# Order of VectorE's additions and one-hots in the edge-counting stage of a two-layer graph network, and who makes one source one-hot of three

## The chip, the cores and the metric

The kernel runs on one core of one Trainium2 chip. The metric is the device time of one execution in microseconds (us). The engines are TensorE (PE in the rows), VectorE (DVE), ScalarE (ACT), GpSimd (POOL) and SyncE (SP), which issues DMAs. They run side by side and meet at semaphores.

## The reference

1250 nodes with 512 features, 20,000 edges sorted by destination. Two layers, cut to what matters here:

```python
h = relu(layernorm(x))
agg = segment_sum(h[src], dst)                 # layer 0
z = (1 + eps) * h + agg
x = x + h + relu(bn(relu(bn(z @ W1 + b1)) @ W2 + b2))
h = relu(layernorm(x))                         # layer 1
m = mish(mish([h[src], h[dst], edge_attr] @ W1 + b1) @ W2 + b2)
agg = segment_sum(m, dst)
x = x + layernorm_affine(h + mish([h, agg] @ W3 + b3) @ W4 + b4)
```

The change lies in how layer 0's aggregation is prepared. The kernel does not gather rows for it: it counts how many edges run from each node to each node, as a matrix, and later multiplies that matrix with h.

## The kernel before

The kernel's stages follow one another: counting the edges (to about 111 us), the product of counts and features, the two batch-normalised products of layer 0, the tables of layer 1, the edge loop of layer 1 (most of the time), and the output products. Nothing of the product of counts and features starts before all counts are added.

**Counting.** The edges are cut into tiles of 128, four tiles to a group, 40 groups (`GROUPS`). One tile contributes a matrix product of two one-hot matrices: a **source one-hot** (128 edges x 128, which of 128 low source numbers the edge has) and a **key one-hot** (128 edges x 400). The key is the high part of the source number times 40 plus the distance of the destination from the lowest one of its half group; so two tiles (a half) give a 128x400 block of counts in a PSUM bank, and that block is added into `edge_counts` at a column offset that is read from memory into a register.

Who makes what, for each group `n`:
- VectorE makes the key one-hots of three tiles (`MADE` = 3): `key_hots`, line 1638, in 16-bit floats.
- GpSimd makes the source one-hots of the same three: `src_hots`, line 558.
- ScalarE makes both one-hots of the fourth tile, in three operations (lines 1185, 1186, 1192), and in 20 of the groups from n = 8 on also writes a layer-norm row of h (line 1199, `ROWS_AT`).
- TensorE multiplies: two tiles into one bank, two into another (line 798), four matmuls of 400 columns, then raises `counted`.
- VectorE adds the two banks into `edge_counts` (`add_counts`, line 1682). The second addition waits for the first by the semaphore `counts_added`, since their columns can overlap. A register operation (line 1681) precedes each, and one load of two words from `lowest_row` (`load_stretch`, line 1543) precedes the group.

One-hots, banks and registers stand in three slots (`SLOT` = 3): the one-hots of group n may be written once group n-3 is counted. VectorE's loop over n, in order: load the stretch of n; the key one-hots of n+2; the additions of n. Other work is hung into this loop at numbers: layer-norm statistics for the first four n (`ln_stats`, lines 1491 and 1495), their reciprocal at n = 6 (`SCALE_AT`), three sums for the tables at n = 11 (`SUMS_AT`, `table_sums`), a split of h into a high and a low part at n = 12 and 15 (line 1733), a check for wide groups at n = 30 (`ANY_AT`, lines 1749 and 1750), and at n = 37 (`MORE_AT`) a branch for groups that cover more columns (`count_more`), not taken here.

**GpSimd's tables.** Between its source one-hots GpSimd works out, for all groups at once, which node tiles they cover. It does a piece behind the one-hots of n = 3, 5, 7 and 9. Behind n = 11 comes `ranges_of_groups`, which waits for VectorE's three sums, and behind n = 13 `tables_ready`, which raises `range_ready`; SyncE then sends the table through DRAM to where VectorE reads it at n = 30. GpSimd's queue is in order: the one-hots of n = 12 stand behind that wait.

The lines around the sums, of GpSimd and of VectorE:

```python
if n == TABLES_AT + 4 * TABLES_STEP:      # GpSimd, n = 11, behind src_hots(n)
    ranges_of_groups()
...
if n == SUMS_AT:                          # VectorE, n = 11, behind key_hots(n + 2)
    table_sums()
```

Of the kernel before, what the change touches and what calls it, by code (L numbers as in the profile page):

```python
# [17 lines left out]
ALU = mybir.AluOpType  # L18
# [8 lines left out]
P = 128  # L27
# [3 lines left out]
NP = NT * P  # L31
KD = DIM // P
KH = HID0 // P
GROUP = 4
RING = 4
TILES = -(-EDGES // (GROUP * RING * P)) * GROUP * RING
GROUPS = TILES // GROUP
# [8 lines left out]
HALVES = 2  # L46
DW = 40
KEYS = NT * DW
MADE = GROUP - 1
# [9 lines left out]
SLOT = 3  # L59
# [4 lines left out]
TABLES_AT, TABLES_STEP, TABLES_SUMMED = 3, 2, 18  # L64
SUMS_AT, ANY_AT = 11, 30
# [4 lines left out]
MORE_AT = GROUPS - 3  # L70
# [38 lines left out]
def gnn_kernel(nc, x, src_cols, dst_cols, dst_rows, edge_attr_t, eps, cols, rows, w01, w02,  # L109
               w1, w2, w3, w4, out):  # L110
    ctx = ExitStack()
    with ctx:
# [3 lines left out]
        def sb(name, shape, dt=F32, at=None):  # L116
            size = 2 if dt in (F16, I16) else 4
            for n in shape[1:]:
                size *= n
            if at is None:  # L120
                at = place[0]
                place[0] += size + (-size) % 32
            return nc.alloc_sbuf_tensor_at(name, shape, dt, offset=at), at + size + (-size) % 32
# [82 lines left out]
        KEY, at = sb("key", [P, TILES], at=at)  # L206
# [5 lines left out]
        LO_F, HI_F = SRC_F[:, 0, :], SRC_F[:, 1, :]  # L212
# [10 lines left out]
        KHOT, at = sb("key_onehot", [P, SLOT, MADE, KEYS], F16, at=wa_at)  # L223
        SHOT, at = sb("src_onehot", [P, SLOT, MADE, P], F16, at=at)
# [4 lines left out]
        IOTA_H, at = sb("iota_half", [P, KEYS], F16, at=at)  # L229
# [123 lines left out]
        def sem(name):  # L353
            return ctx.enter_context(nc.semaphore(name))
# [11 lines left out]
        src_ready, key_ready, src_hot, key_hot, hot_act, distance_made = (sem(n) for n in  # L366
            ("src_ready", "key_ready", "src_hot", "key_hot", "hot_act", "distance_made"))
        counted, counts_added, x_added, h0_hi, h0_lo = (sem(n) for n in
            ("counted", "counts_added", "x_added", "h0_hi", "h0_lo"))
# [165 lines left out]
        def _(pool):  # L535
# [17 lines left out]
            def src_hots(n):  # L553
                if n >= SLOT:
                    pool.wait_ge(counted, n - SLOT + 1)
                for j in range(MADE):
                    t = GROUP * n + j
                    ins = nc.gpsimd.tensor_scalar(SHOT[:, n % SLOT, j, :], IOTA[:, 0:P], LO_F[:, t:t + 1], None, ALU.is_equal)
                ins.then_inc(src_hot, 1)
# [7 lines left out]
            def lowest_and_highest():  # L567

                pool.wait_ge(extremes_made, 2)
                table(nc.gpsimd.tensor_copy(RNG_G[:, R_MIN:R_MIN + HALVES], LOW2[:, :]))  # L570
                table(nc.gpsimd.tensor_scalar(ENDS[:, 0:1], LOW2[:, 0:1], LOW2[:, 1:2], None, ALU.min))
                table(nc.gpsimd.tensor_scalar(ENDS[:, 1:2], HIGH2[:, 0:1], HIGH2[:, 1:2], None, ALU.max))
                table(nc.gpsimd.tensor_tensor(SPAN[:, :], HIGH2[:, :], LOW2[:, :], ALU.subtract))
                pairs = [GROUPS, HALVES, HALVES * GROUPS]
                table(nc.gpsimd.tensor_tensor(NEAR[:, 0, :, :], LOWS[:, :].rearrange("g (o k) -> g o k", o=1).broadcast_to(pairs),
                                              LOW2[:, :].rearrange("g (h o) -> g h o", o=1).broadcast_to(pairs), ALU.subtract))

            def stretches():

                pool.wait_ge(table_made, steps[0])  # L580
                table(nc.gpsimd.tensor_tensor(WIDTH[:, :], ENDS[:, 1:2], ENDS[:, 0:1], ALU.subtract))
                for h in range(HALVES):
                    table(nc.gpsimd.tensor_scalar(PASSED[:, h, :], NEG_DW[0:GROUPS, 1:MORE_MAX + 1], SPAN[:, h:h + 1], 0.0, ALU.add, ALU.is_ge))
                for k in range(2):
                    table(nc.gpsimd.tensor_scalar(TILES_BELOW[:, k, :], NEG_TILE[:, :], ENDS[:, k:k + 1], 0.0, ALU.add, ALU.is_ge))
                table(nc.gpsimd.tensor_scalar(NEAR[:, 1, :, :], NEAR[:, 0, :, :], 0.0, None, ALU.is_le))

            def first_tiles():

                pool.wait_ge(table_made, steps[0])
                table(nc.gpsimd.tensor_scalar(MULTI[:, :], WIDTH[:, :], float(P), None, ALU.is_ge))
                table(nc.gpsimd.tensor_scalar(ONE_TILE[:, :], WIDTH[:, :], float(P), None, ALU.is_lt))
                table(nc.gpsimd.tensor_scalar(NEXT[:, :], ENDS[:, 0:1], float((NT - 1) * P), None, ALU.is_lt))
                table(nc.gpsimd.tensor_scalar(NEAR[:, 0, :, :], NEAR[:, 0, :, :], -float(DW), None, ALU.is_gt))

            def further_tiles():

                pool.wait_ge(table_made, steps[0])  # L600
                table(nc.gpsimd.tensor_scalar(NEXT[:, :], NEXT[:, :], 2.0, -1.0, ALU.mult, ALU.add))
                table(nc.gpsimd.tensor_tensor(NEAR[:, 0, :, :], NEAR[:, 0, :, :], NEAR[:, 1, :, :], ALU.mult))
                assert steps[0] == TABLES_SUMMED, steps
# [21 lines left out]
            for n in range(GROUPS):  # L625
                src_hots(n)
                if n == TABLES_AT:
                    lowest_and_highest()
                if n == TABLES_AT + TABLES_STEP:
                    stretches()  # L630
                if n == TABLES_AT + 2 * TABLES_STEP:
                    first_tiles()
                if n == TABLES_AT + 3 * TABLES_STEP:
                    further_tiles()
                if n == TABLES_AT + 4 * TABLES_STEP:
                    ranges_of_groups()
                if n == TABLES_AT + 5 * TABLES_STEP:
                    tables_ready()


# [71 lines left out]
            for s in range(SLOTS, EDGE_PAIRS):  # L712
# [7 lines left out]
                if W3_PAIR <= s < W3_PAIR + 2 * W3_PIECES:  # L720
                    n = (s - W3_PAIR) // 2
# [753 lines left out]
        def _(dve):  # L1475
# [59 lines left out]
            range_regs = [[dve.alloc_register(f"dve_range{n}_{j}") for j in range(2 * HALVES)] for n in range(SLOT)]  # L1535
# [93 lines left out]
            link(nc.vector.tensor_copy(MIN_ROW[:, :], lows[0:1, :]))  # L1629
            nc.vector.tensor_copy(LOWS[:, :], lows[0:GROUPS, :]).then_inc(extremes_made, 1)  # L1630

            def key_hots(n):

                if n >= SLOT:
                    dve.wait_ge(counted, n - SLOT + 1)
                for j in range(MADE):
                    t = GROUP * n + j
                    ins = nc.vector.tensor_scalar(KHOT[:, n % SLOT, j, :], IOTA_H[:, :], KEY[:, t:t + 1], None, ALU.is_equal)  # L1638
                ins.then_inc(key_hot, 1)

            dve.wait_ge(pool_const, 4)
            dve.wait_ge(key_ready, 1)
            for n in range(2):
                key_hots(n)

            def counts_at(first):
                return COUNTS[:, :, bass.ds(first, DW)]

            def counted_in(bank):
                return BANKS[:, bank, 0:KEYS].rearrange("p (c w) -> p c w", w=DW)  # L1650

            def counts_more(n, half):

                past = dve.snap(range_regs[0][HALVES + half], min_val=0, max_val=MORE_MAX)
                with dve.If(past > 0):
                    low = dve.snap(range_regs[0][half], min_val=0, max_val=NP - 1)
                    with dve.Fori(0, past) as k:
# [13 lines left out]
                        nc.vector.tensor_tensor(counts_at(first), counts_at(first), counted_in(XBANK), ALU.add).then_inc(xagg_done, 1)  # L1671
                        dve.reg_add(extras, extras, 1)

            def add_counts(n):

                g = n % SLOT
                dve.wait_ge(counted, n + 1)
                for half in range(HALVES):
                    if half or n > 0:
                        dve.wait_ge(counts_added, HALVES * n + half)  # L1680
                    first = dve.snap(range_regs[g][half], min_val=0, max_val=NP - 1)
                    nc.vector.tensor_tensor(counts_at(first), counts_at(first), counted_in(2 * g + half), ALU.add).then_inc(counts_added, 1)  # L1682

            def spare_rows():

# [80 lines left out]

            for n in range(GROUPS):
                load_stretch(n % SLOT, n)
                if n + 2 < GROUPS:
                    key_hots(n + 2)  # L1770
                if n == MORE_AT:
                    count_more()
                if n == SUMS_AT:
                    table_sums()
                if n == ANY_AT:
                    any_range()
                add_counts(n)
                if n < LG:
                    dve.wait_ge(x_in[n], 16)
                    ln_stats(X, n)  # L1780
                if n == SCALE_AT:
                    dve.wait_ge(std_ready, LG)
                    link(nc.vector.reciprocal(RSTD[:, 0:NT], TMP[:, 4, 0:NT]))
                    nc.vector.scalar_tensor_tensor(NBIAS[:, 0:NT], LN_MV[:, 0:NT, 0], -1.0, RSTD[:, 0:NT],
                                                   ALU.mult, ALU.mult).then_inc(scale_ready, LG)
                if n in SPLIT_AT:
                    split_h0(SPLIT_AT.index(n))
# [106 lines left out]
            for q, (a, b) in enumerate(FILLS):  # L1894
# [9 lines left out]
                for nt in range(a, b):  # L1904
                    dve.wait_ge(dve_chain, chain[0] - (b - 1 - nt))
                    ins = nc.vector.bn_aggr(LN_MV[:, nt, :], STATS[:, nt, :])
# [285 lines left out]
```

## Time and profile before

| | us |
|---|---|
| median of 3 runs | 1142.43 (1142.24 to 1142.64) |
| the profiled execution | 1142.65 |
| its span, first to last instruction | 1140.84 |
| first additions of counts | 11.47 |
| cast of the finished counts begins | 110.84 |

How to read it: a row of the timeline has the start and the length of a run of equal instructions on one engine, and in brackets how long the engine had been idle before and what ended that. A row's length is that of the instruction in the engine's pipeline; the next may start before it has ended, so what a cycle takes is read from starts. Instructions of an engine's sequencer (register operations, loads into registers) carry a q behind the engine's name.

### The profile page before, as it was taken

The page shows a single profiled execution, that of the slowest core. Times are in us where ns is not written, and L with a number is a line of the kernel's source. Part 1 is how long each engine was busy: PE and PEld are TensorE (multiplying, and loading weights), DVE is VectorE, ACT ScalarE, POOL GpSimd, SP SyncE. Part 2 cuts the span into 40 slices and gives each one's busy share as a digit, 9 for nine tenths or more (in the row PEclk, how much of TensorE's full clock was granted, in tenths as well). Part 3 has the DMA queues.
Part 4 walks back from the last instruction along what each step waited for, and adds up shares of the span by engine and source line. Part 5 has one row for each costly group of instructions (what it writes and reads, how often), then busy time and mean ns, then how long its engine had stood idle before and what let it go on. Part 6 is the DMA issues. An engine that isn't in the chain of part 4 may idle for free.

```text
span 1140.8 us, 18418 instructions
## 1 busy us (share of the span) xinstructions
PE 1061.1 (93%) x5689; PEld 893.8 (78%) x5690; DVE 875.8 (77%) x1489; ACT 898.0 (79%) x1134; POOL 676.5 (59%) x589
## 2 busy tenths in 40 slices
PE   3565999998999999999999999999999999999897
PEld 1121889998788888888888888888888888888695
DVE  7798626544525388888899899989988888888786
ACT  6795745633621699999999999999999999999584
POOL 8696505000335487767788888888877677660217
PEclk7556999999899999999999999999999999999899
DMA  2000940110165477666676666666666666761002
GB/s 102 8 1 24 194 101 15 48 74 24 69 210 117 89 169 164 133 138 134 138 136 130 138 139 134 136 139 133 133 145 133 135 138 134 140 126 42 1 1 90
DMA packets 61087, 121.40 MB, mean 106 GB/s; under 512 B 7851, under 2 KB 18348, under 8 KB 60918
## 3 DMA queue, kind: packets, MB, share of 16 engines
q0 software_dynamic: 38048, 87.58, 38.9%
q1 hardware_dynamic: 22998, 33.32, 8.8%
q8 instruction: 20, 0.33, 0.1%
q14 instruction: 21, 0.17, 0.0%
HBM read 107.82 MB, written 7.80 MB: 101 GB/s over the span
## 4 chain that ended last, share of the span: by engine, by line
PE 85%; DVE 10%; issue 2%; POOL 1%; ACT 1%; DVEq 1%; ACTq 0%; POOLq 0%
PE banks L1032 12%; PE banks L1027 12%; PE banks L1028 12%; PE banks L932 10%; PE banks L1012 7%; PE banks L1049 6%; PE banks L1006 6%; PE banks L975 5%; PE banks L855 4%; PE banks L994 4%; DVE edge_counts L1682 3%; PE banks L1025 3%; DVE key_onehot L1638 2%; PE banks L1109 2%; PE banks L909 1%
## 5 line engine op out<-in xcount | busy, mean ns | idle before, releaser
L681 POOL DMA_INDIRECT gather_pq<-q_table,dst x157 | 295.6, 1883 | 56.9 <-issue 47.5
L673 POOL DMA_INDIRECT gather_pq<-p_table,src x157 | 173.0, 1102 | 137.2 <-PE banks L1012 84.0
L1027 PE MATMUL banks<-w_lo,h_hi 128*128 128x512 f32 x620 | 241.5, 389 | 0.0
L1028 PE MATMUL banks<-w_hi,h_hi 128*128 128x512 f32 x620 | 241.3, 389 | 0.0
L1032 PE MATMUL banks<-w_hi,h_lo 128*128 128x512 f32 x620 | 166.2, 390 | 0.0
L1028 PEld LDWEIGHTS banks<-w_hi,h_hi 128*128 128x128 f32 x620 | 116.4, 188 | 24.8
L1032 PEld LDWEIGHTS banks<-w_hi,h_lo 128*128 128x128 f32 x620 | 116.4, 188 | 24.2
L1958 DVE SCALAR_TENSOR_TENSOR h_full<-mish_work,banks 128x512 f32<-128x512 f32 (+1 forms) x154 | 98.5, 681 | 46.6 <-ACT mish_work L1336 43.9
L1027 PEld LDWEIGHTS banks<-w_lo,h_hi 128*128 128x128 f32 x620 | 116.5, 188 | 21.9
L1983 DVE SCALAR_TENSOR_TENSOR message<-mish_work,banks 128x1024 f32<-128x1024 f32 x78 | 95.3, 1222 | 8.7 <-ACT mish_work L1360 0.7
L1324 ACT ACTIVATE mish_work<-banks 128x1024 f32<-128x1024 f32 (+1 forms) x77 | 78.7, 1022 | 26.2 <-PE banks L1012 26.2
L1012 PE MATMUL banks<-edge_attr_parts,we_hi 128*128 128x256 f32 (+1 forms) x316 | 94.5, 321 | 2.1 <-DVE edge_attr_parts L1951 2.1
L1993 DVE TENSOR_TENSOR message_lo<-message,message_hi 128x1024 fp32r<-128x1024 f32 x78 | 96.1, 1232 | 0.1
L1006 PE MATMUL banks<-ident,gather_pq 128*128 128x128 f32 x628 | 94.4, 272 | 0.6 <-DMA gather_pq<-q_table,dst 0.3
L1972 DVE TENSOR_TENSOR h_lo<-h_full,h_hi 128x1024 fp32r<-128x1024 f32 (+1 forms) x77 | 93.3, 1212 | 0.0
L798 PE MATMUL banks<-key_onehot,src_onehot 128*128 128x400 f16 x120 | 44.0, 495 | 46.5 <-DVE key_onehot L1638 32.7
L1356 ACT ACTIVATE mish_work<-mish_work 128x1024 f32<-128x1024 f32 (+1 forms) x79 | 83.4, 1056 | 2.5
L1006 PEld LDWEIGHTS banks<-ident,gather_pq 128*128 128x128 f32 x628 | 74.8, 140 | 11.5 <-DVE h_full L1958 0.6
L1332 ACT ACTIVATE mish_work<-mish_work 128x1024 f32<-128x1024 f32 (+1 forms) x77 | 81.4, 1057 | 2.4
L1328 ACT ACTIVATE mish_work<-mish_work 128x1024 f32<-128x1024 f32 (+1 forms) x77 | 81.3, 1056 | 2.5
L1360 ACT ACTIVATE mish_work<-mish_work 128x1024 f32<-128x1024 f32 (+1 forms) x79 | 83.1, 1052 | 0.1
L1352 ACT ACTIVATE mish_work<-mish_work 128x1024 f32<-128x1024 f32 (+1 forms) x79 | 82.4, 1044 | 0.1
(266 smaller groups left out, 2720.2 us busy)
## 6 DMA issues: line engine op xcount, KB each, us to landing
edge_attr<-in_edge_attr_t SPq DMA_DIRECT2D x79, 128.0 KB, 3.6
x_nodes<-h_hi POOLq DMA_DIRECT2D x10, 256.0 KB, 12.4
x_nodes<-h_lo POOLq DMA_DIRECT2D x10, 256.0 KB, 7.9
p_table<-p_stage SPq DMA_DIRECT2D x10, 256.0 KB, 2.0
q_table<-agg_nodes SPq DMA_DIRECT2D x10, 256.0 KB, 2.9
gather_pq<-p_table,src POOLq DMA_INDIRECT x157, 3.9
gather_pq<-q_table,dst POOLq DMA_INDIRECT x157, 5.2
x_nodes<-in_x SPq DMA_DIRECT2D x3, 768.0 KB, 7.0
```

The costliest lines, as they stand in the source:

```text
L673: nc.gpsimd.indirect_dma_start(GP[:, 2 * j + k, :], None, p_tab[:, :], bass.IndirectOffsetOnAxis(ap=SRC[:, 2 * s + k:2 * s + k + 1], axis= ...
L681: nc.gpsimd.indirect_dma_start(GP[:, 2 * j + k, :], None, q_tab[:, :], bass.IndirectOffsetOnAxis(ap=DST[:, 2 * s + k:2 * s + k + 1], axis= ...
L932: mm = pe.matmul(bank, weights[w][:, k, o * P:(o + 1) * P], acts[a](k)[:, nodes], start=(k == 0 and n == 0), stop=(k == kn - 1 and n == 2) ...
L1006: pe.matmul(Z1v[:, c, k * P:(k + 1) * P], GP[:, 2 * slot + k, c * P:(c + 1) * P], IDENT[:, :], is_transpose=True, skip_group_check=True, s ...
L1012: mm = pe.matmul(Z1v[:, c, 0:P * tiles(s)], w[:, c * P:(c + 1) * P], AT_R[:, j, 0:P * tiles(s)], skip_group_check=True, start=False, stop= ...
L1027: pe.matmul(at, h_high(s, j)[:, c, e], W2_LO[:, c, :], start=False, stop=False)
L1028: pe.matmul(at, h_high(s, j)[:, c, e], W2_HI[:, c, :], start=False, stop=False)
L1032: mm = pe.matmul(at, h_low(s, j)[:, c, e], W2_HI[:, c, :], start=False, stop=(c == KD - 1))
L1958: nc.vector.scalar_tensor_tensor(h_full_of(s)[:, at[0], at[1]], z1_work(s)[:, at[0], at[1]], -0.5, Z1v[:, at[0], at[1]], ALU.add, ALU.mult ...
L1972: nc.vector.tensor_tensor(h_low(s, j)[:, :, 0:P * tiles(s)], h_full_of(s)[:, :, 0:P * tiles(s)], h_high(s, j)[:, :, 0:P * tiles(s)].bitcas ...
L1983: nc.vector.scalar_tensor_tensor(MSG[:, :, :], EB[:, :, :], -0.5, z2_out(s, j), ALU.add, ALU.mult).then_inc(msg_full, 1)
L1993: nc.vector.tensor_tensor(MSG_LO[:, :, :], MSG[:, :, :], MSG_HI[:, :, :].bitcast(F32), ALU.subtract).then_inc(msg_lo, 1)
```

## The change

1. GpSimd makes the source one-hots of two tiles of a group instead of three. VectorE makes the third (`src_last`), in 16-bit floats from `iota_half` instead of from the 32-bit `iota`. The semaphore `key_hot` is raised behind it.
2. For n below 37, VectorE's loop no longer makes the key one-hots of n+2 ahead of the wait for group n's counts. It waits for the counts first and then alternates: first addition of n, one key one-hot of n+2, second addition of n, two key one-hots and the source one-hot of n+2. From n = 37 the order is as it was.
3. GpSimd calls `ranges_of_groups` behind n = 15 and `tables_ready` behind n = 17, where it was 11 and 13.

```diff
             def src_hots(n):
...
-                for j in range(MADE):
+                for j in range(MADE - 1):
...
-                if n == TABLES_AT + 4 * TABLES_STEP:
+                if n == SUMS_AT + SLOT + 1:
+
                     ranges_of_groups()
-                if n == TABLES_AT + 5 * TABLES_STEP:
+                if n == SUMS_AT + SLOT + 1 + TABLES_STEP:
                     tables_ready()
...
+            def key_one(n, j):
+                t = GROUP * n + j
+                nc.vector.tensor_scalar(KHOT[:, n % SLOT, j, :], IOTA_H[:, :], KEY[:, t:t + 1], None, ALU.is_equal)
+
+            def src_last(n):
+                t = GROUP * n + MADE - 1
+                nc.vector.tensor_scalar(SHOT[:, n % SLOT, MADE - 1, :], IOTA_H[:, 0:P], LO_F[:, t:t + 1], None, ALU.is_equal).then_inc(key_hot, 1)
+
             def key_hots(n):
 
                 if n >= SLOT:
                     dve.wait_ge(counted, n - SLOT + 1)
                 for j in range(MADE):
-                    t = GROUP * n + j
-                    ins = nc.vector.tensor_scalar(KHOT[:, n % SLOT, j, :], IOTA_H[:, :], KEY[:, t:t + 1], None, ALU.is_equal)
-                ins.then_inc(key_hot, 1)
+                    key_one(n, j)
+                src_last(n)
...
+            def add_between_hots(n):
+
+
+                dve.wait_ge(counted, n + 1)
+                add_half(n, 0)
+                key_one(n + 2, 0)
+                add_half(n, 1)
+                for j in range(1, MADE):
+                    key_one(n + 2, j)
+                src_last(n + 2)
...
             for n in range(GROUPS):
                 load_stretch(n % SLOT, n)
-                if n + 2 < GROUPS:
+                if MORE_AT <= n < GROUPS - 2:
                     key_hots(n + 2)
...
-                add_counts(n)
+                if n < MORE_AT:
+                    add_between_hots(n)
+                else:
+                    add_counts(n)
```

`add_half(n, half)` is the body of the old loop in `add_counts`: the wait for `counts_added`, the register operation and the addition.

On VectorE, one turn of the loop around group 10 and the next one's load, before (ISA is the register operation of line 1681):

```order
L1543 TENSOR_LOAD lowest_row
L1638 TENSOR_SCALAR key_onehot<-iota_half,key 128x400 x3
L1681 ISA
L1682 TENSOR_TENSOR edge_counts<-edge_counts,banks 128x10x40
L1681 ISA
L1682 TENSOR_TENSOR edge_counts<-edge_counts,banks 128x10x40
L1543 TENSOR_LOAD lowest_row
```

The same turn now:

```order
L1544 TENSOR_LOAD lowest_row
L1687 ISA
L1688 TENSOR_TENSOR edge_counts<-edge_counts,banks 128x10x40
L1635 TENSOR_SCALAR key_onehot<-iota_half,key 128x400
L1687 ISA
L1688 TENSOR_TENSOR edge_counts<-edge_counts,banks 128x10x40
L1635 TENSOR_SCALAR key_onehot<-iota_half,key 128x400 x2
L1639 TENSOR_SCALAR src_onehot<-iota_half,src_parts 128x128
L1544 TENSOR_LOAD lowest_row
```

One hot has moved between the additions, two behind them, and the source one-hot stands ahead of the next load.

On GpSimd, from the last piece of the early tables (behind n = 9) to `tables_ready`, before:

```order
L602 TENSOR_TENSOR lowest_near<-lowest_near 40x160
L558 TENSOR_SCALAR src_onehot<-iota,src_parts 128x128 x6
L608 CAST range_groups<-tile_of 40x1
...
L613 TENSOR_SCALAR range_groups<-reached_by 40x2
L558 TENSOR_SCALAR src_onehot<-iota,src_parts 128x128 x6
L618 TENSOR_SCALAR range_groups<-extra_tiles,many_tiles 40x1
```

And now:

```order
L602 TENSOR_TENSOR lowest_near<-lowest_near 40x160
L558 TENSOR_SCALAR src_onehot<-iota,src_parts 128x128 x12
L608 CAST range_groups<-tile_of 40x1
...
L613 TENSOR_SCALAR range_groups<-reached_by 40x2
L558 TENSOR_SCALAR src_onehot<-iota,src_parts 128x128 x4
L618 TENSOR_SCALAR range_groups<-extra_tiles,many_tiles 40x1
```

The six one-hots of n = 10 and 11 ahead of the wait have become twelve, of n = 10 to 15.

## Rows read from the trace of the kernel before

**Rows 1.** Timeline: start, length, engine; additions of n0, n4, n11, n12, n36; cast.

```profile
11.47 1.29 DVE L1682 TENSOR_TENSOR edge_counts<-edge_counts,banks 128x400 f32 x2
...
29.15 1.27 DVE L1682 TENSOR_TENSOR edge_counts<-edge_counts,banks 128x400 f32 x2
...
45.28 1.27 DVE L1682 TENSOR_TENSOR edge_counts<-edge_counts,banks 128x400 f32 x2
...
50.44 1.29 DVE L1682 TENSOR_TENSOR edge_counts<-edge_counts,banks 128x400 f32 x2 [3.04 <-PE banks L798]
...
103.76 1.28 DVE L1682 TENSOR_TENSOR edge_counts<-edge_counts,banks 128x400 f32 x2
...
110.84 1.26 ACT L1229 CAST counts_hi<-edge_counts 128x1280 fp32r<-128x1280 int16 x1 [9.54 <-DVE edge_counts L1682]
```

**Rows 2.** Chain of waits, 60 to 106 us, shares by line.

```profile
by line: DVE edge_counts L1682 47.9%; DVE key_onehot L1638 35.6%; issue 10.4%; DVEq L1681 4.9%; DVE any_more L1749 0.8%; DVEq L1543 0.7%; DVEq L1757 0.7%; DVEq L1759 0.2%; DVE any_more L1750 0.1%
```

**Rows 3.** One stretch: busy us of PE, PEld, DVE, ACT, POOL, clock, DMA.

```profile
60.60:103.70 43.10, 26.99 (x80) 8.11 (x80) 39.24 (x103) 35.93 (x69) 38.76 (x64) 0.63 0.00 1
```

**Rows 4.** Chain of waits, pieces in order: start, length; GpSimd idle.

```profile
42.13 0.13 DVE key_onehot L1638
42.37 0.55 DVE key_onehot L1638 x2
42.92 0.49 DVE edge_counts L1682
43.55 0.55 DVE edge_counts L1682
44.15 0.22 DVE key_onehot L1638
```

**Rows 5.** Timeline, VectorE: an addition and the independent operation behind it.

```profile
33.90 0.57 DVE L1682 TENSOR_TENSOR edge_counts<-edge_counts,banks 128x400 f32 x1
34.39 0.21 DVE L1783 RECIPROCAL rstd<-tmp 128x10 f32<-128x10 f32 x1
```

**Rows 6.** The loads (ns min/median/max), one register operation, the hot at 44.62.

```profile
L1543 DVEq TENSOR_LOAD <-lowest_row x40: 523/528/781, 9.6 to 108.8; - x40
...
L1681 DVEq FUSED_REGOPS  x1: 55/55/55, 44.4 to 44.4; - x1
...
44.62 0.32 DVE key_onehot L1638
```

**Rows 7.** Timeline: GpSimd's wait for the sums and TensorE's for its hots.

```profile
45.43 0.18 POOL L608 CAST range_groups<-tile_of 40x1 int32<-40x1 f32 x1 [8.14 <-DVE reached_by L1743]
...
48.80 1.16 PE L798 MATMUL banks<-key_onehot,src_onehot 128*128 128x400 f16 x3 [6.25 <-POOL src_onehot L558]
```

**Rows 8.** Other work on VectorE: splits, a reduction, a late load.

```profile
L1733 DVE TENSOR_TENSOR h_lo<-h_nodes,h_hi 128x512 fp32r<-128x512 f32 x2 | 1.4, 684 | 0.0
...
90.47 0.42 DVE L1749 TENSOR_REDUCE any_more<-tile_range 1x4 int32<-1x160 int32 x1
...
85.05 0.33 DVEq L1543
```

**Rows 9.** All key one-hots: ns min/median/max, first and last start.

```profile
L1638 DVE TENSOR_SCALAR key_onehot<-iota_half,key x120: 303/338/656, 7.7 to 105.5; 128x400 f16<-128x400 f16 x120
```

**Rows 10.** Timeline, TensorE: the four matmuls of one group.

```profile
97.69 1.16 PE L798 MATMUL banks<-key_onehot,src_onehot 128*128 128x400 f16 x3 [0.53 <-DVE key_onehot L1638]
98.65 0.51 PE L798 MATMUL banks<-both_onehots 128*128 128x400 f16 x1
```

**Rows 11.** Timeline, VectorE: statistics, hots behind a load, a slow trio.

```profile
22.50 1.87 DVE L1491 BATCH_NORM_STATS2 stats<-x_nodes 128x6 f32<-128x512 f32 x3
...
25.00 0.81 DVE L1638 TENSOR_SCALAR key_onehot<-iota_half,key 128x400 f16<-128x400 f16 x3 [0.41 <-issue]
...
35.31 1.58 DVE L1638 TENSOR_SCALAR key_onehot<-iota_half,key 128x400 f16<-128x400 f16 x3 [0.43 <-PE banks L798]
```

**Rows 12.** Chain of waits: twelve matmuls of the next stage, twice.

```profile
112.25 4.31 PE banks L855 x12
...
119.25 2.35 PE banks L855 x12
```

More of the change, by code:

```diff
@@ L1672, in counts_more, with add_half @@
                         dve.reg_add(extras, extras, 1)
+            def add_half(n, half):
+                g = n % SLOT
+                if half or n > 0:
+                    dve.wait_ge(counts_added, HALVES * n + half)
+                first = dve.snap(range_regs[g][half], min_val=0, max_val=NP - 1)
+                nc.vector.tensor_tensor(counts_at(first), counts_at(first), counted_in(2 * g + half), ALU.add).then_inc(counts_added, 1)
             def add_counts(n):
-                g = n % SLOT
                 dve.wait_ge(counted, n + 1)
                 for half in range(HALVES):
[L1679 to L1682, printed above, removed]
+                    add_half(n, half)
+            def add_between_hots(n):
[6 more added lines that the diff above has]
+                src_last(n + 2)
             def spare_rows():
```

## The prediction

> **What bounds the kernel now.** Only the counting stage is changed, so I read that alone: it runs from the first addition at 11.47 us to the cast of the finished counts at 110.84 [rows 1]. Everything later waits for its end. The chain of waits names the engine: between 60 and 106 us the chain is VectorE's additions (47.9%) and VectorE's key one-hots (35.6%) [rows 2]. TensorE is busy 26.99 of 43.10 us there, ScalarE 35.93, GpSimd 38.76, VectorE 39.24 [rows 3]. So what counts is VectorE's **cycle per group**: one load of the stretch, three key hots, two additions.
>
> Next the cycle, piece by piece, where GpSimd stands idle [rows 4]: key hot to next hot 0.24 (42.13 to 42.37), the other two hots and the start of the addition to 42.84 or so, then 0.49 of addition, a gap, 0.55 of addition, a gap, next cycle at 44.15. The cycle is 2.02. Two things in it are idle waiting. The second addition waits for the semaphore of the first: an addition begins 0.71 after the other although whatever is independent of it may begin 0.49 after it (33.90 to 34.39) [rows 5]. And the next cycle's first hot begins 0.60 after the second addition, since the load of the next stretch takes 0.53 [rows 6] and the hots are queued behind it.
>
> Last, where the stage isn't at its cycle. GpSimd's table of ranges waits 8.14 us for VectorE's sums, with the source hots of group 12 queued behind it; TensorE starves 6.25 us and VectorE's additions of group 12 come at 50.44, 3.04 us idle before them, after those of group 11 at 45.28 [rows 1, 7].
>
> **The change part by part.** I use the 40 groups, n = 0 to 39, and the starts of their first additions [rows 1]: n0 11.47, n4 29.15, n11 45.28, n12 50.44, n36 103.76.
>
> *The new cycle.* Addition, one key hot, addition, two key hots, the source hot. Spacings: 0.49 after an addition, 0.24 after a hot. The second addition still needs the first one's semaphore, 0.71 after it; the hot in between fills 0.49 + 0.24 = 0.73, so that wait costs 0.02 at most. The source hot is not in the trace in this form; it has 128 columns where a key hot has 400. Its spacing lies between a third of 0.24, 0.08, and the whole, 0.24; I take the middle, 0.16. Sum: 0.49 + 0.24 + 0.49 + 0.24 + 0.24 + 0.16 = 1.86 against 2.02. The load hides if VectorE's sequencer runs ahead of the engine: issued behind the source hot, but while the second addition still runs. The row for it: the register operation of group 11's addition stands at 44.4, behind three hots and three reductions in the program, while the third hot began only at 44.62 [rows 6]. It had passed four instructions that had not begun; the new order asks it to pass three.
>
> *GpSimd beside it.* Before, the 24 cycles from n12 to n36 take 53.32 us. They hold 2.2 us of other work: two splits of 0.68, of which 0.6 each counts, 0.65 for the two reductions of any_range (0.42 the first), 0.35 for one late load [rows 8]. That leaves 2.13 a cycle, 0.11 over the clean 2.02, with GpSimd making three source hots of 38.76/64 = 0.61 us. The wait shows in the hots too: 303 ns at least, 338 in the median, 656 at most [rows 9]. With two hots on GpSimd I take two thirds of it, 0.08. **New cycle: 1.94 us.**
>
> *The others must keep up.* TensorE: hots made at 97.55, matmuls from 97.69 to 99.16 at half clock [rows 10], then 0.14 from its semaphore to an addition, as between two additions (42.84 + 0.57 to 43.55). VectorE now makes group n+2's hots only after group n is counted, so two cycles must cover 0.14 + 1.47 + 0.14 and one whole chain of VectorE's own, 1.86: 3.61 against 3.88. It fits by 0.27. ScalarE is busy 35.93/20 = 1.80 a group, GpSimd now 2 x 0.61 = 1.22 plus tables. All below 1.94.
>
> *n4 to n12*, before 21.29 us. Now 8 x 1.94 = 15.52, the three reductions of table_sums 0.42 (hots end their spacing at 44.86, addition at 45.28), and the two small operations of the layer-norm scale: 0.92 from 34.39 to 35.31, plus 0.17, because an exposed load is now followed by the register operation and its 0.1 us to the addition instead of by hots. 15.52 + 0.42 + 1.09 = 17.03: **4.25 us gained**. The stall of rows 7 is in it: the table is asked for behind the hots of group 15, and the sums are made by then, since hots 15 need group 12 counted and the sums precede the additions of group 11. What is late next there is nothing but the cycle. The six table operations (45.43 to 46.8) lie beside VectorE; range_ready moves later but is needed only at n30 and at the stage's end.
>
> *n12 to n36*, before 53.32. Now 24 x 1.94 + 2.2 = 48.76: **4.56 gained**.
>
> *n0 to n4*, before 17.68. Four cycles each lose 0.15 by the exposed load (statistics at 22.50, hots at 25.00 with 0.41 idle [rows 11]), 0.6 in all; against that the slow trio of hots at 15.19 may go, 0.9. The first addition stays at 11.47, where TensorE's first group ends. Between -0.6 and +0.3 with the trio kept or gone; a trio as slow stands at 35.31 (1.50 rather than 0.71) [rows 11], and if that goes too, 0.8 more comes back. **0.2 gained**.
>
> *The end*, n36 to 110.84: hots of 39 and a source hot more, nearly hidden behind the loads of count_more: **0.2 lost**.
>
> Sum: 4.25 + 4.56 + 0.2 - 0.2 = **8.8 us**. The profiled execution took 1142.65 (span 1140.84), the median is 1142.43; 8.8 off the median gives 1133.6.
>
> *TensorE's clock.* The next stage starts at half clock: twelve matmuls 4.31 us from 112.25, 2.35 later at full clock [rows 12]. Where the grant falls after an earlier start is open: about one such 1.96 either way. I put 0 and keep 1.9 in the range.
>
> **The rivals.** *The cycle decides, and its break-even can be stated:* 32 cycles carry the 8.8, so 1.94 + 8.8/32 = 2.215 us is the cycle at which nothing is gained.
>
> (a) **The load is exposed.** If the load goes out only when the source hot starts, a cycle has 0.53 + 0.05 + 0.17 = 0.75 where I put 0.16: 2.53 us. 32 x (2.53 - 2.215) = 10.1 us slower, 1152.5. It decides from an exposure of 0.28 on. Against it stands the register operation that ran ahead; for it, the exposed loads after the statistics, but those follow instructions that wait. 5%.
>
> (b) **Hots blocked by GpSimd.** Hots now start after an addition twice a cycle, not once. If each such start waits for the rest of a running GpSimd operation, half of 0.61 at a presence of 1.22/1.94, that is 0.19 each, 0.38 a cycle: 2.24 instead of 1.94, which is 1143. Before, one start at a presence of nearly one would cost 0.3 by this, and the rows bear 0.11. The slow trios show it can happen. 6%, and 3% that it locks in for more of the hots and is slower.
> The Trainium skill (SBUF — State Buffer, "SBUF: two separate sides") states this as a rule: the port pair that VectorE and GpSimd share is locked for a whole instruction, and the other engine blocks. By it the sum would be 1143 rather than 1133.6; the trace shows both, blocked trios and unblocked ones.
>
> (c) **The loop over TensorE and ScalarE bites.** With 0.27 of slack, a ScalarE group with a layer-norm row or a delayed source hot can hold the second pair of matmuls, and VectorE, which now waits at the head of the cycle, stands. A cycle of 2.0 to 2.15 gives 1135.5 to 1140.3. 22%.
>
> (d) **Cleaner than I think**: 1.86, no slow trios, an early full clock: 32 x 0.08 + 0.8 + 1.9 is 5.3 more, 1128.3 at most. 9%.
>
> My forecast, cycle 1.86 to 2.0 (1131 to 1135.5): 55%.
>
> **How the numbers follow.** Predicted 1133.6. The range takes the forecast, (c) and the nearer half of (d): 1130.0 to 1140.0; about 19% lies outside. A measurement tells 0.2%, 2.3 us, from no change. Faster: 55 + 9 + nearly all of (c), 85%. Same: 7%. Slower: (a) and the lock of (b), 8%.
>
> **What would show it.** In the new trace: first additions of neighbouring groups 1.9 to 2.0 apart from group 4 to 36, no hole at group 12, no GpSimd wait for the sums; loads inside the second addition; cast of the counts at 102 us. Wrong if idle time by issue stands before every first addition (a), if hots last 0.6 (b), or if additions wait for matmuls (c); and the sum is wrong in its source-hot term if that operation spaces more than 0.24.

## The result

| | median us | runs |
|---|---|---|
| before | 1142.54 | 1142.24 to 1145.13, 4 runs |
| changed | 1133.50 | 1132.90 to 1133.70, 4 runs |

The ratio is 0.9908, with a 95% interval of 0.9891 to 0.9925: 9.0 us less. The profiled execution of the changed kernel took 1133.70 us, its span is 1131.7 (1140.8 before). The forecast was 1133.6. The two parts that make up that agreement were both off, by about 2 us each and in opposite directions; most of what follows is about them.

### The profile page after: what moved, and what is told of

It is laid out like the page before. It is cut to its first block, busy times and chain, and to the rows that moved or that the text cites. A ratio compares the mean times of both kernels' runs of the same rounds, so it can differ in the third digit from the quotient of the medians.

```text
span 1131.7 us, 18418 instructions
## 1 busy us (share of the span) xinstructions
PE 1063.5 (94%) x5689; PEld 896.5 (79%) x5690; DVE 871.2 (77%) x1529; ACT 896.6 (79%) x1134; POOL 656.5 (58%) x549
## 4 chain that ended last, share of the span: by engine, by line
PE 86%; DVE 9%; ACT 2%; issue 2%; DVEq 1%; POOL 0%; ACTq 0%; POOLq 0%
PE banks L1033 12%; PE banks L1028 12%; PE banks L1029 12%; PE banks L933 10%; PE banks L1013 7%; PE banks L1050 6%; PE banks L1007 6%; PE banks L976 5%; PE banks L856 4%; PE banks L995 4%; DVE edge_counts L1688 4%; PE banks L1026 3%; PE banks L1110 2%; DVE key_onehot L1635 1%; PE banks L910 1%
## 5 line engine op out<-in xcount | busy, mean ns | idle before, releaser
L1325 ACT ACTIVATE mish_work<-banks 128x1024 f32<-128x1024 f32 (+1 forms) x77 | 78.6, 1021 | 26.3 <-PE banks L1013 26.3
L1349 ACT ACTIVATE mish_work<-banks 128x1024 f32<-128x1024 f32 (+1 forms) x79 | 79.2, 1003 | 3.3 <-PE banks L1033 3.3
```

## The profile after

Timeline of the changed kernel: the first additions of n0, n4, n11, n12 and n36, and the cast of the counts (start, length, engine), to be laid beside [rows 1]:

```profile
11.46 0.57 DVE L1688 TENSOR_TENSOR edge_counts<-edge_counts,banks 128x400 f32 x1 [1.67 <-PE banks L799]
...
28.64 0.57 DVE L1688 TENSOR_TENSOR edge_counts<-edge_counts,banks 128x400 f32 x1 [0.59 <-issue]
...
43.52 0.55 DVE L1688 TENSOR_TENSOR edge_counts<-edge_counts,banks 128x400 f32 x1
...
45.37 0.56 DVE L1688 TENSOR_TENSOR edge_counts<-edge_counts,banks 128x400 f32 x1
...
92.48 0.56 DVE L1688 TENSOR_TENSOR edge_counts<-edge_counts,banks 128x400 f32 x1
...
99.72 1.26 ACT L1230 CAST counts_hi<-edge_counts 128x1280 fp32r<-128x1280 int16 x1 [7.26 <-DVE edge_counts L1688]
```

The cast starts at 99.72 instead of 110.84: **the counting stage is 11.1 us shorter**, not 8.8. The hole at n12 is gone (1.85 us from n11 instead of 5.16). The 0.59 us of idle before the addition of n4 is the load and the register operation behind the statistics.

One whole cycle of VectorE, same view:

```profile
60.02 0.56 DVE L1688 TENSOR_TENSOR edge_counts<-edge_counts,banks 128x400 f32 x1
60.50 0.31 DVE L1635 TENSOR_SCALAR key_onehot<-iota_half,key 128x400 f16<-128x400 f16 x1
60.73 0.56 DVE L1688 TENSOR_TENSOR edge_counts<-edge_counts,banks 128x400 f32 x1
61.21 0.55 DVE L1635 TENSOR_SCALAR key_onehot<-iota_half,key 128x400 f16<-128x400 f16 x2
61.68 0.24 DVE L1639 TENSOR_SCALAR src_onehot<-iota_half,src_parts 128x128 f16<-128x128 f16 x1
61.88 0.57 DVE L1688 TENSOR_TENSOR edge_counts<-edge_counts,banks 128x400 f32 x1
```

Starts: 0.48, 0.23, 0.48, 0.47 for two, 0.20: 1.86. VectorE is without a gap. The loads still take their 0.53; this one is issued at 60.9, behind three instructions that hadn't begun, and ends before the next cycle:

```profile
L1544 DVEq TENSOR_LOAD <-lowest_row x1: 527/527/527, 60.9 to 60.9; - x1
...
L1635 DVE TENSOR_SCALAR key_onehot<-iota_half,key x120: 305/314/429, 7.7 to 94.8; 128x400 f16<-128x400 f16 x120
```

The second row answers [rows 9]: minimum, median and maximum of a key one-hot were 303, 338 and 656 ns and are 305, 314 and 429. No key one-hot takes 0.6 us any more. A little is left elsewhere: one source one-hot took 0.51 us, at 34.05.

Busy time by stretch (PE, PEld, DVE, ACT, POOL, then TensorE's granted clock, where 1.00 is full and 0.50 half, then DMA), first of the kernel before, then of the changed one: the start of the next stage up to where its half clock ends, and a piece behind the table products:

```profile
110.80:116.10 5.30, 3.85 (x11) 3.30 (x12) 4.23 (x12) 4.47 (x6) 4.97 (x9) 0.50 0.72 230
...
356.00:359.80 3.80, 3.80 (x28) 3.80 (x28) 3.80 (x7) 1.36 (x3) 3.23 (x2) 1.00 0.45 67
```
```profile
99.70:107.20 7.50, 6.08 (x17) 5.09 (x18) 6.45 (x15) 5.59 (x7) 7.20 (x10) 0.55 0.87 237
...
356.40:359.80 3.40, 3.40 (x16) 3.40 (x15) 0.00 (x0) 1.07 (x2) 2.34 (x3) 0.50 0.95 219
```

Before, the next stage ran at half clock up to 116.1, which covers 3.85 us of its matmuls; now half clock lasts from 100.4 to 107.2, which covers 6.08 us of them, and another half-clock piece of 3.4 us has appeared at 356. That is where the rest of the 11.1 went. The chain of waits follows it; before, then changed (start, length, matmuls):

```profile
112.25 4.31 PE banks L855 x12
...
166.79 60.92 PE banks L932 x420
...
291.45 5.46 PE banks L975 x12
...
367.61 10.36 PE banks L994 x72
379.79 6.89 PE banks L994 x48
```
```profile
101.12 4.61 PE banks L856 x12
106.05 2.96 PE banks L856 x12
...
156.73 60.92 PE banks L933 x420
...
281.40 4.54 PE banks L976 x12
...
356.58 12.02 PE banks L995 x72
370.43 6.89 PE banks L995 x48
```

The lead is 11.13 us at the first matmul of the stage (112.25 - 101.12), 10.06 where the next product starts, 9.36 at 379.79 against 370.43, and 9.1 at the end of the span. In between, it had grown again to 11.0 (first matmul of line 994 at 352.36, of 995 at 341.34), as the half clock around the batch-norm pause (286.7 to 297 before, 274.5 to 284.7 now) covers less of the matmuls behind it: the first twelve of line 976 take 4.54 us where those of line 975 took 5.46.

A caution on the page of the changed kernel: it shows full clock from the start, but its clock records begin only at 86.8 us. The matmuls tell: a group's four take 1.5 us at 60 us, half clock, and 0.84 at 92.7, full clock.

## The experiments

Two theories. **A**: VectorE's cycle decides until another engine is slower; the order takes two idle waits out of it, the source one-hot costs its spacing. **B**: the gain comes from GpSimd, which is relieved of a third of its work and disturbs VectorE less. The second question, on top of them, is who took 2 us back. All kernels are compared with the kernel before on the same chip, whose median there was 1143.8 to 1144.1. "Stage" is the start of the cast of the counts in the one profiled execution, which no later clock can blur. Two kernels were profiled twice, and their stages repeat to 0.2 us (99.72 and 99.75, 98.56 and 98.36); but the same groups can also take a few tenths more in another execution, as in warm_tail below. The edits are shown against the changed kernel, those of source_only and tables_only against the kernel before.

### The parts, one by one

**order_only**: the new order on VectorE alone; the table calls at 11 and 13, and on GpSimd:

```diff
-                for j in range(MADE - 1):
+                for j in range(MADE):
...
-                if n == SUMS_AT + SLOT + 1:
+                if n == TABLES_AT + 4 * TABLES_STEP:
```


> Of the change only the new order of additions and key one-hots on VectorE; GpSimd makes three source one-hots, its tables stay behind n = 11 and 13. Theory A (VectorE's cycle decides): VectorE's own work is 1.70 us a group, so GpSimd with three source one-hots of 0.61 (1.83, plus its tables) sets about 1.87 a group where it runs free; the stall behind the sums at n = 11 stays and is now paid in full, since GpSimd has no lead to give back: 1136 to 1139 us. Theory B (the gain is GpSimd's relief): the order alone brings little, cycle 2.0 or more, 1140 or more.

Measured 1135.13 (1133.83 to 1136.93), ratio 0.9918; stage 101.91. So the order alone gives 8.9 of the 11.1 us. A, though the median is 0.9 below A's 1136 to 1139. The hole at n12 stays (5.21 us from n11). GpSimd with three one-hots keeps up, as its own timeline of this kernel says: eleven without a break, 0.62 each, 1.87 a group:

```profile
61.67 6.86 POOL L558 TENSOR_SCALAR src_onehot<-iota,src_parts 128x128 f16<-128x128 f32 x11
```

**order_tables**: as order_only, but with the later table calls (the changed kernel without the moved source one-hot, so GpSimd makes three).

```diff
-                src_last(n + 2)
...
-                for j in range(MADE - 1):
+                for j in range(MADE):
```


> New order and later tables, but GpSimd still makes all three source one-hots. Theory A: GpSimd's 1.83 plus its tables sets the cycle, 1.86 to 1.9 against 1.86 in the changed kernel: 1133 to 1135.5 us, so the moved source one-hot is worth little. Theory B: the moved one-hot is what pays, and without it 1137 or more with idle time of TensorE before GpSimd's one-hots.

Measured 1132.53 (1129.34 to 1133.91), ratio 0.9890; stage **98.56, 1.2 us earlier than the changed kernel**. The moved one-hot does not pay. (The median is 0.5 below A's range.)

**source_only**: the third source one-hot on VectorE behind the three key one-hots, two on GpSimd; order and tables as before.

```diff
                 for j in range(MADE):
                     key_one(n, j)
+                src_last(n)
```


> Only the third source one-hot moved to VectorE; old order, old places of the tables. Theory A: VectorE's cycle grows by the one-hot's spacing, 0.16 by my sum: 2.18 plus what contention is left, 1144 to 1147 us less one or two for the shorter stall at n = 12, as GpSimd catches up with two one-hots a group. Theory B: relief of GpSimd outweighs it, 1141 or less.

Measured 1145.68 (1145.32 to 1147.36), ratio 1.0017 (1.0005 to 1.0028); stage 113.78, 2.9 later than before. Most cycles are 2.17 to 2.18, that is 2.02 and 0.16. Over the 24 cycles from n12 to n36, less the 2.2 of other work, 0.04 is left on top where the kernel before had 0.11. A: the relief of GpSimd takes 0.07 off a cycle, but the one-hot costs 0.16.

**tables_only**: only the two calls moved.

```diff
-                if n == TABLES_AT + 4 * TABLES_STEP:
+                if n == SUMS_AT + SLOT + 1:
```


> Only the two calls of GpSimd's tables moved to n = 15 and 17. Both theories: the hole at n = 12 goes. By my sum it is worth the 5.15 us cycle of group 12 less a plain one of 2.1, and 0.5 to 1 of late one-hots behind it: 1138.3 to 1139.5 us. A rival: the table work behind n = 15 costs the same later, because GpSimd with three one-hots (1.83 of 2.1) has no room for it: 1141 or more.

Measured 1139.35 (1137.96 to 1142.59), ratio 0.9968; stage 106.91, 3.9 earlier. n11 to n12 takes 2.02 instead of 5.16.

**tables_early**: the changed kernel with the calls back at 11 and 13.

```diff
-                if n == SUMS_AT + SLOT + 1:
+                if n == TABLES_AT + 4 * TABLES_STEP:
```


> The changed kernel with GpSimd's two table calls back behind n = 11 and 13. If the later calls are what closes the hole at n = 12: the sums come at 43.6 us, GpSimd then needs 1.4 for its tables and 1.2 for two one-hots, TensorE 0.15 and 1 to 1.5, so the additions of group 12 come 4.0 to 4.5 behind those of group 11 instead of 1.85, and the stage and the kernel lose 2.0 to 2.7 us against the changed kernel (1133.5), two thirds of what the hole cost with three one-hots. If the relief of GpSimd closes the hole by itself: no loss.

Measured 1136.15 (1135.03 to 1139.21), ratio 0.9938; stage 103.39, 3.7 later; the kernel loses 2.65, inside the range, but the additions of n12 come 4.79 behind those of n11, more than the 4.0 to 4.5 expected. The profile of the hole, in this kernel, GpSimd's relief notwithstanding:

```profile
45.33 2.35 POOL L558 TENSOR_SCALAR src_onehot<-iota,src_parts 128x128 f16<-128x128 f32 x4
46.62 1.16 PE L798 MATMUL banks<-key_onehot,src_onehot 128*128 128x400 f16 x3 [3.69 <-POOL src_onehot L558]
...
48.26 0.57 DVE L1687 TENSOR_TENSOR edge_counts<-edge_counts,banks 128x400 f32 x1 [2.89 <-PE banks L798]
```

The tables wait for VectorE's sums, the one-hots of n12 wait for the tables, TensorE idles 3.69 us, VectorE 2.89. The later calls are needed; two one-hots instead of three don't close it.

Stage ends side by side:

| source one-hot | order before, tables early | order before, tables late | new order, tables early | new order, tables late |
|---|---|---|---|---|
| on GpSimd | 110.84 | 106.91 | 101.91 | 98.56 |
| on VectorE | 113.78 | not run | 103.39 | 99.72 |

The order is worth 8.3 to 10.4, the later tables 3.3 to 3.9, the moved one-hot **costs** 1.2 to 2.9. B falls as the source of the gain.

### The disputed terms of the sum

**source_two**: two of the three source one-hots on VectorE, one on GpSimd.

```diff
-                for j in range(MADE - 1):
+                for j in range(MADE - 2):
...
+                for j in (MADE - 2, MADE - 1):
```


> The changed kernel with two of three source one-hots on VectorE, GpSimd makes one. It measures the term that I put at 0.16 us. If VectorE's cycle is the bound: it grows from 1.86 by one source one-hot's spacing, 0.16 to 0.2, to 2.02 to 2.06, 32 cycles, 5 to 6.5 us more than the changed kernel. If GpSimd's share slows VectorE's hots noticeably, its relief gives part back and the cycle stays under 2.0.

Measured 1138.21 (1136.16 to 1138.85), ratio 0.9950; stage 104.72. The cycle in the timeline, addition to addition:

```profile
60.23 0.56 DVE L1690 TENSOR_TENSOR edge_counts<-edge_counts,banks 128x400 f32 x1
...
61.90 0.41 DVE L1640 TENSOR_SCALAR src_onehot<-iota_half,src_parts 128x128 f16<-128x128 f16 x2
62.22 0.56 DVE L1690 TENSOR_TENSOR edge_counts<-edge_counts,banks 128x400 f32 x1
```

1.99, below the 2.02 to 2.06 expected if nothing came back from GpSimd's relief. But the other spacings are those of the changed kernel's cycle to 0.01 (0.49, 0.23, 0.48, 0.47), so nothing came back; the second source one-hot is cheaper than I took it: two of them space 0.32, where one spaced 0.20 in the cycle shown and 0.16 in others. My 0.16 stands as the mean of two.

**load_exposed**: the changed kernel, but the sequencer must see its source one-hot finished before it issues the next load, n from 5 to 37.

```diff
+                if 5 <= n <= MORE_AT:
+                    dve.wait_ge(key_hot, n + 2)
                 load_stretch(n % SLOT, n)
```


> The changed kernel, but from n = 5 to 37 VectorE's sequencer waits for its own last source one-hot before it issues the load of the next stretch: the prediction's rival (a) made real. If the load is hidden today only because the sequencer runs ahead: each cycle grows from 1.86 by the one-hot's end, its semaphore, 0.53 of load and 0.2 of register operation, less 0.2 of spacing, about 0.8; 32 x 0.8 = 26 us more, 1156 to 1161. If the load is not really hidden today and partly paid already: under 10 us more.

Measured 1160.79 (1160.46 to 1163.18), ratio 1.0144; stage 129.13, 29.4 later. Chain of waits of this kernel between two cycles:

```profile
59.78 0.53 DVEq L1544
60.31 0.05 issue
60.36 0.02 DVEq L1686
60.38 0.05 issue
60.43 0.06 DVEq L1687
60.48 0.05 issue
60.53 0.57 DVE edge_counts L1688
```

0.75 us from the load to the addition, just the exposure that rival (a) was priced with; the cycle is 2.84 (60.53 to 63.37). It shows what the run-ahead of VectorE's sequencer is worth: about 1 us a cycle. The groups without a split of h have the same 2.84. The break-even that I gave, a cycle of 2.215, comes out roughly: (2.84 - 2.215) x 32 = 20, and the kernel is 17 us slower than the one before, its stage 18.3 later.

### Who took 2 us back

**warm_tail**: 16 small matmuls of constants behind the last group, their result unused.

```diff
             for n in range(GROUPS):
                 count_group(n, n % SLOT)
+            for _ in range(16):
+                pe.matmul(BANKS[:, LOW_BANK, 0:P], ONES_R[:, :].bitcast(F32), IOTA[:, 0:P], start=True, stop=True)
```


> The changed kernel with 16 small matmuls of constants (128 columns of 32 bits) on TensorE behind the last counted group, into a bank that nobody reads. In the changed kernel TensorE idles 4.9 us there at full granted clock and the chip falls to half clock from 100.4 to 107.2 us. If that idle stretch is what drops the clock, and the drop is what eats most of the 11.1 us that the counting stage gains: full clock stays over the start of the next stage, 6.1 us at half clock become about 3.3, 2.5 to 3 us less than the changed kernel. If the clock falls for another reason, or the gain is lost elsewhere: no change, or some tenths more because matmuls stand in the queue.

Measured 1132.49 (1131.59 to 1133.95), ratio 0.9902. The stage ended 0.7 us later in the profiled run (100.46), most of it in the groups from 29 to 32, before the added matmuls; why is not shown. And yet that run was 2.1 us faster than the changed kernel's (1131.59 against 1133.70). Its next stage starts with matmuls at full clock, 0.23 and 0.11 apart, where the changed kernel had 0.43 and 0.19 (the row of the added 16 counts 32, two to each):

```profile
97.90 4.36 PE L829 MATMUL banks<-iota,ones 128*128 128x128 f32 x32
102.01 0.48 PE L858 MATMUL banks<-counts_hi,h_hi 128*128 128x512 f32 x1
102.33 0.39 PE L858 MATMUL banks<-counts_hi,h_lo 128*128 128x512 f32 x1
102.56 0.27 PE L858 MATMUL banks<-counts_hi,h_hi 128*128 128x232 f32 x1
102.67 0.28 PE L858 MATMUL banks<-counts_hi,h_lo 128*128 128x232 f32 x1
```

The medians, of two chips, don't separate it from the changed kernel (1133.50), and 1.0 less is not the 2.5 to 3 that I expected. The profile shows only that the half clock at the stage's start and at 356 is gone; what that is worth, order_tables_warm shows below.

**pad_test**: the changed kernel with a clear of 1280 columns ahead of the last additions.

```diff
+                if n == GROUPS - 1:
+                    nc.vector.memset(A_HI[:, 2, 0:1280].bitcast(F32), 0.0)
```


> The changed kernel with one idle clear of 1280 columns on VectorE ahead of the last group's additions, about 1.3 us on the stage's chain, nothing else. If time moves one to one: 1.3 us more. If the granted clock's place is what decides the rest: the following stages start at another place against the chip's changes of clock, and the end moves by something else, 0 to 3 us more, with the half-clock stretches (100 to 107 and 356 to 360) at other places or gone.

Measured 1133.53 (1132.75 to 1136.32), ratio 0.9912. The stage ends 1.73 later (101.45; the clear is 1.1 of it, most of the rest stands in slower cycles of groups 24 to 26), and the profiled run takes 1133.71, as without it (1133.70). Its first twelve matmuls took 4.41 and the next were at full clock at once, and the half-clock piece at 356 is missing:

```profile
102.85 4.41 PE banks L856 x12
107.43 2.35 PE banks L856 x12
```

So the kernel's end does not follow the stage's end one to one: the 1.7 us came back entirely, through the clock.

### The changed kernel again, and a better one

Three kernels on one chip, five, five and four executions. **after_again** is the changed kernel, **order_tables_again** the one with all source one-hots on GpSimd, **order_tables_warm** that one with the 16 matmuls of warm_tail.

> The changed kernel once more, on the chip of the next three kernels. 0.990 to 0.993 of the kernel before; counting stage finished at 99.7 us, whatever the granted clock does behind it.

> The changed kernel with all three source one-hots back on GpSimd, beside the changed kernel. If the moved one-hot is worth nothing (GpSimd's 3 x 0.61 = 1.84 a group against VectorE's 1.86 with it): counting stage finished at 98.6 us against 99.7, and a median 0 to 1.5 us below the changed kernel's. If its one profile on the other chip was luck: the same or above.

> New order, later tables, three source one-hots on GpSimd, and 16 small matmuls of constants on TensorE behind the last counted group. If both findings add up: 1.2 us from the stage and 1 to 2.5 from the kept clock, 2 to 3.5 us under the changed kernel. If the clock's drop comes back behind the table products (around 355 us), only 1.

| | median us | runs | ratio to before | stage |
|---|---|---|---|---|
| after_again | 1133.71 | 1133.49 to 1135.16 | 0.9913 (0.9896 to 0.9930) | 99.75 |
| order_tables_again | 1132.06 | 1129.68 to 1133.73 | 0.9896 (0.9875 to 0.9916) | 98.36 |
| order_tables_warm | 1128.19 | 1127.67 to 1128.85 | 0.9860 (0.9841 to 0.9880) | 98.48 |

The second repeats: the stage is 1.4 us shorter, the median 1.65 lower; four of its five runs lie below the changed kernel's fastest, but the intervals overlap, so in total time that step is likely and not proven. The third is clearly ahead, 5.5 us below the changed kernel, and its runs lie closest together. Its direct comparison is order_tables_again, the same kernel without the 16 matmuls: 3.9 us less in the median, and no run of one lies among those of the other. Its TensorE in the tail, in the timeline (start, length):

```profile
95.32 3.73 PE L829 MATMUL banks<-iota,ones 128*128 128x128 f32 x32
99.89 0.47 PE L858 MATMUL banks<-counts_hi,h_hi 128*128 128x512 f32 x1 [0.83 <-ACT counts_hi L1232]
```

And the busy time of the stretch from there on (PE, PEld, DVE, ACT, POOL, granted clock, DMA):

```profile
98.50:107.20 8.70, 7.87 (x45) 6.69 (x45) 7.62 (x19) 7.50 (x10) 8.43 (x10) 1.00 0.85 236
```

Idle time ahead of the next stage is 0.83 us instead of 4.9 (3.9 in order_tables_again), and the clock is 1.00 throughout where it was 0.55. The product after it starts at 152.65 against 156.73: 4.1 us, of which 1.2 are the stage and 2.8 the clock. Against order_tables_again, whose stage ends within 0.1 us of it, that product starts 2.7 earlier (155.35), which is the clock alone. The half-clock piece at 356 is gone too. I expected 2 to 3.5 us in all; it was 5.5.

## Why the prediction was right, and where it was right by luck

**The cycle, step by step.** The clean sum of 1.86 came out as 1.86; its terms of 0.49, 0.24 and 0.16 came out to 0.01, but for the source one-hot, 0.16 to 0.20. **Wrong was the term for GpSimd, 0.08.** I scaled a contention of 0.11 by the number of one-hots. With two one-hots on GpSimd it measures 0.01 over the cycles from n12 to n36 (47.11 less 2.2 of other work is 24 x 1.87): key one-hots take 314 ns in the median and 429 at most (338 and 656 before [rows 9]), and most cycles are 1.86. source_two, with one, has 1.99, and 1.99 - 1.86 is the added one-hot and nothing else. It is not the new order that took the contention away: in order_tables, the new order with three on GpSimd, key one-hots take 342 ns in the median and 764 at most, and source_only, the old order with two, has 0.04 left of the 0.11. So most of it goes with the third one-hot, more than the third of it that I took; why so is not shown by any run. With three on GpSimd in the new order most cycles are 1.83 to 1.87, but there GpSimd is the bound.

**By stretches.** n4 to n12: forecast 17.03, measured 45.37 - 28.64 = 16.73; the cycles gave more, but the scale's two small operations at n = 6 took 1.35 over a plain cycle and not 1.09. n12 to n36: forecast 48.76, measured 47.11; the 1.65 are 24 cycles of 0.07. n0 to n4: 0.5 gained, not 0.2, as the slow trio at 15.19 went and an exposed load cost 0.07 to 0.09 where I took 0.15. The end: 0.16 lost, 0.2 forecast. Together 11.1 instead of 8.8.

**The stall.** Right in mechanism: the hole is gone and nothing is late in its place. tables_only prices it at 3.9 us of the stage, tables_early at 3.7.

**The load.** Right: hidden by the sequencer's run-ahead. load_exposed confirms the 0.75 of rival (a), though a cycle lost 0.98 and not the 0.59 above my 1.94, since that kernel also waits for the one-hot's end.

**The clock: the step that failed and hid the first error.** I put it at 0 with 1.9 either way, "about one such 1.96". The lead shrank by 2.0: 1.1 at the start of the next stage, some 1.7 near 356, 0.3 behind that without a place that I can name, less 1.0 regained at 275 to 285. warm_tail, pad_test and order_tables_warm show that this is the granted clock: where TensorE's idle time is filled or the stage's end shifted, the loss changes or goes, with the stage the same or even longer. I had priced the first place at 1.96 either way, where 1.1 was lost, and had not looked at the second at all: a wait of TensorE for VectorE stands there in both kernels (2.1 us ahead of line 1012, 2.6 ahead of the same line, now 1013), and only the changed one had the clock fall behind it. So the total of 1133.6 was right by luck: 2.3 us too little for the stage and 2.0 too little for the clock.

**The rivals.** (a) no. (b) no: a key one-hot of up to 656 ns before, while GpSimd was at work, agrees with the Trainium skill's rule (SBUF — State Buffer, "SBUF: two separate sides") that one of the two engines blocks for the other's whole instruction, and in the 8.14 us in which GpSimd stood idle no trio was slow; but the wait did not strike at each start after an addition, which would have made 2.24 of the cycle. (c) no: TensorE waits for the one-hots, 0.3 to 0.4 us in most groups at half clock, near the 0.27 of slack; VectorE waited for a matmul in the stage twice. (d) happened to the stage, at 1.86 without slow trios, and the clock took back 2.0 of it.

**What the prediction did not ask.** Whether each part earns its place. It summed the cycle with the source one-hot in it; without it the same rows give 0.49 + 0.24 + 0.49 + 0.24 + 0.24 = 1.70 for VectorE and 3 x 0.61 = 1.83 for GpSimd, a cycle of 1.83 to 1.85, below 1.86. That was there to be read ahead.

## What to carry to other kernels

Between two dependent operations of one engine put an independent one that is needed anyway: here it filled a semaphore wait of 0.2 us and hid a register load, and made a chain of 40 groups 8 to 10 us shorter. Before moving work off a busy neighbour, compare both engines' cycles after the move: GpSimd at 1.83 a group was no bound until VectorE went below it, and VectorE with the work added stood at 1.86. And when a stage ahead of dense matmuls gets shorter, look at TensorE's idle time in front of them: the granted clock can take back a fifth of the gain, and a few unused matmuls in the gap bring it back.

## What the runs showed of the hardware that I had not expected

- A shortening of 11.1 us in one stage was worth 9.1 at the end, and a lengthening of 1.7 us was worth 0.0, through the placement of half-clock stretches of the granted clock 6.8 and 3.4 us long, one of them 250 us later.
- Sixteen fp32 matmuls of 128 columns in TensorE's idle time (3.9 us without them) kept the following stage's start at clock 1.00, worth 2.7 us there and 3.9 us in all.
- VectorE's sequencer passes instructions that have not begun: in the changed kernel the load is issued at 60.9, when the second addition had started at 60.73 and the operations at 61.21 to 61.68 stood between them. Forbidding that, with a wait for the last one's end, cost 0.98 us a cycle.
- A 16-bit source one-hot of 128 columns costs VectorE 0.13 to 0.20 us, GpSimd's from 32 bits 0.62. With three of them on GpSimd a cycle of the kernel before held 0.11 us of contention; with two there it held 0.04 in the old order and 0.01 in the new.
